# Attention over a dense adjacency mask: a fifth of the eight key groups is turned by DMA instead of TensorE, with SP's loads put ahead of its turns

## What is computed

```python
q = x @ Wq.T + bq;  k = x @ Wk.T + bk;  v = x @ Wv.T + bv
scores = jnp.where(adj > 0, q @ k.T / sqrt(128), -9e15)
att = softmax(scores, axis=-1) @ v
return layernorm(x + elu(att))          # no scale or shift, eps 1e-5
```

## Time and profile before

| | |
|---|---|
| median of 3 runs | 428.43 us |
| the profiled execution, its own time | 429.13 us |
| its span, first to last instruction | 427.3 us |
| TensorE busy | 416.2 us (97% of the span) |
| VectorE, ScalarE, GpSimd busy | 360.8, 353.8, 354.0 us |
| granted TensorE clock, mean | 0.998 |
| bytes moved by DMA | 104.77 MB, mean 245 GB/s |
| first and last turn issued by SP | 36.3 and 413.0 us |
| last load of adj issued | 386.4 us |

### The profile page before, as it was taken

How to read it: one execution, slowest core, us unless ns; L and a number is a source line. 1 busy time by engine, 2 the same in 40 slices (tenths; PEclk the granted TensorE clock), 3 DMA queues, 4 the chain that set the end, 5 groups by cost and what they waited for, 6 DMA issues and landing times.

```text
span 427.3 us, 11462 instructions
## 1 busy us (share of the span) xinstructions
PE 416.2 (97%) x3470; PEld 311.3 (73%) x3470; DVE 360.8 (84%) x677; ACT 353.8 (83%) x742; POOL 354.0 (83%) x644
## 2 busy tenths in 40 slices
PE   7997999999999999999999999999999999999994
PEld 6764777767777777777777777777777777777784
DVE  3889988888888898888888988888889888888784
ACT  4987788888888889888888898888888988888892
POOL 0596578988898889888988898889888988898875
PEclk9999999999999999999999999999999999999999
DMA  8944999899999999999999999999999999998550
GB/s 253 399 161 111 266 275 251 208 294 263 286 268 254 275 264 267 238 280 266 259 251 280 268 265 244 272 271 263 245 277 271 256 250 271 263 267 225 104 103 21
DMA packets 149794, 104.77 MB, mean 245 GB/s; under 512 B 132755, under 2 KB 141461, under 8 KB 141717
## 3 DMA queue, kind: packets, MB, share of 16 engines
q1 hardware_dynamic: 149344, 104.41, 92.0%
q10 hardware_dynamic: 436, 0.20, 0.2%
HBM read 69.47 MB, written 2.10 MB: 167 GB/s over the span
## 4 chain that ended last, share of the span: by engine, by line
POOL 58%; issue 18%; PE 10%; DMA 4%; ACT 3%; DVE 2%; POOLq 2%; SPq 2%; ACTq 0%; DVEq 0%
POOL p_rows L409 26%; POOL res L423 5%; POOL var_eps L445 4%; POOL rstd L447 4%; POOL att_sum L416 3%; POOL y L428 3%; POOL neg_mean L434 3%; POOL att L418 3%; POOL centred L436 2%; POOL expm L425 2%; DMA p_turned<-p_rows 2%; PE ps_out L967 2%; POOL y_out L451 2%; DMA x_rows<-in_x_dram 2%; POOL var L443 1%
## 5 line engine op out<-in xcount | busy, mean ns | idle before, releaser
L409 POOL TENSOR_TENSOR p_rows<-scores,p_rows 128x256 f16<-128x256 f32 x252 | 177.0, 733 | 7.3 <-ACT p_rows L566 7.1
L696 DVE CUSTOM_DVE_ANT_0 scores<-ps_scores,adj 128x1024 f32<-128x1024 f32 x128 | 155.9, 1218 | 13.0 <-issue 9.3
L549 ACT ACTIVATE scores<-scores,neg_max 128x1024 f32<-128x1024 f32 x128 | 145.8, 1139 | 3.5 <-DVE neg_max L706 3.5
L712 DVE TENSOR_TENSOR p_lo<-ps_t,p_hi 128x512 f16<-128x512 f32 x124 | 82.6, 686 | 28.4 <-ACT p_hi L558 28.3
L682 DVE TENSOR_SCALAR adj<-adj 128x1024 f32<-128x1024 int32 x128 | 103.5, 810 | 0.2
L928 PE MATMUL ps_scores<-k_hi,q_hi 128*128 128x512 f16 x256 | 97.0, 379 | 0.5 <-DVE max_parts L696 0.5
L929 PE MATMUL ps_scores<-k_lo,q_hi 128*128 128x512 f16 x256 | 97.0, 379 | 0.0
L930 PE MATMUL ps_scores<-k_hi,q_lo 128*128 128x512 f16 x256 | 97.0, 379 | 0.0
L967 PE MATMUL ps_out<-v_parts,p_turned 128*128 128x256 f16 x496 | 95.0, 273 | 0.4 <-DMA p_turned<-p_rows 0.3
L967 PE MATMUL ps_out<-v_parts,p_hi 128*128 128x256 f16 x496 | 95.1, 273 | 0.0
L969 PE MATMUL ps_out<-v_parts,p_lo 128*128 128x128 f16 x496 | 88.5, 219 | 0.0
(11 more groups left out here) (121 smaller groups left out, 479.8 us busy)
## 6 DMA issues: line engine op xcount, KB each, us to landing
adj<-in_adj_dram SPq DMA_DIRECT2D x63, 1024.0 KB, 5.3
out_dram<-y_out SPq DMA_DIRECT2D x32, 64.0 KB, 4.9
x_rows<-in_x_dram SPq DMA_DIRECT2D x4, 256.0 KB, 4.4
x_rows<-in_x_dram SPq DMA_DIRECT2D x2, 512.0 KB, 7.6
adj<-in_adj_dram SPq DMA_DIRECT2D x2, 512.0 KB, 7.4
p_turned<-p_rows SPq DMA_TRANSPOSE x63, 4.5
w_rows<-in_L_gnn_Wq_dram ACTq DMA_DIRECT2D x1, 64.0 KB, 2.7
w_rows<-in_L_gnn_Wk_dram ACTq DMA_DIRECT2D x1, 64.0 KB, 3.3
```

What stands on the lines that cost most here:

```text
L409: last = nc.gpsimd.tensor_tensor(p_rows[c][:, w:][:, cols], s_sb[s][:, c * PIECE:c * PIECE + w][:, cols], p_rows[c][:, 0:w][:, cols], ALU. ...
L549: nc.scalar.activation(s_sb[s][:, cols], s_sb[s][:, cols], ACT.Exp, bias=neg_max[:, s:s + 1], accum_out=p_sums[:, s, c:c + 1]).then_inc(ex ...
L696: nc.vector.tensor_tensor_reduce(out=s_sb[s][:, cols], in0=ps_scores[c % 2][:, :], in1=mask_sb[s][:, cols], scale=SCALE, scalar=-3.0e38, o ...
L712: nc.vector.tensor_tensor(p_lo[:, k, :], ps_t[bank_of(s, g)][:, :], p_hi[:, k, :], ALU.subtract).then_inc(plo_ready, 1)
```

## The change

Key group 4 (512 columns) moves from the TensorE way to the DMA way. `DMA_COLS` becomes (1024, 1536), so `p_rows[1]` holds 1536 high and 1536 low columns, and the turn of c = 1 moves 0.79 MB. TensorE's four transposes for group 4, ScalarE's `high_part(4)` and VectorE's `low_part(4)` go. In their place ScalarE makes the high part of the odd 512 columns from SBUF (`high_rows_odd`, step 6), and VectorE their low part from SBUF (`low_rows_odd`, step 7 after `row_max`). The turn of c = 1 waits for GpSimd's `rows_lo` and for VectorE's `rows_lo_odd`. GpSimd's own `low_rows` keep their size. `high_rows` of piece 1 moves from ScalarE's step 6 to step 4. SP's order in a period becomes: load of the second half for tile p+1, turn of c = 1, store, load of the first half for tile p+2, turn of c = 0. VectorE's four mask pieces of a period become pieces 2 and 3 of tile p and 0 and 1 of tile p+1. `PV_ORDER` and `T_AT` are fitted, the last tile keeps group 4 on TensorE.

```diff
-DMA_COLS = (PIECE, PIECE)
+DMA_COLS = (PIECE, PIECE + BANK)
-T_AT = {4: 6, 5: 7, 6: 8, 7: 10}
-PV_ORDER = (4, 0, 5, 6, 1, 7, 2, 3)
+T_AT = {5: 6, 6: 8, 7: 10}
+PV_ORDER = (5, 0, 1, 6, 7, 2, 3, 4)
...
             def turn(i, s, c):
                 sp.wait_ge(rows_lo, BY_DMA * i + c + 1)
                 sp.sem_inc(turn_begun, 1)
+                if c == 1:
+                    sp.wait_ge(rows_lo_odd, i + 1)
+                    sp.sem_inc(turn_begun, 1)
                 sp.dma_start_transpose(p_turned[c][s][:, :, :], p_rows[c][:, :]).then_inc(turned[c], 16)

             def period(p, n, head=True, turns_0=True, turns_1=True, stores=True, loads=True):
+                if head:
+                    load_half(p + 1, 1 - n, 1, False)
                 if turns_1:
                     turn(p - 2, n, 1)
-                if head:
-                    load_half(p + 1, 1 - n, 1, False)
                 if stores:
                     store(p - 4, n)
+                if loads:
+                    load_half(p + 2, n, 0, False)
                 if turns_0:
                     turn(p - 1, 1 - n, 0)
-                if loads:
-                    load_half(p + 2, n, 0, False)
...
+            def high_rows_odd(i, s, first):
+                act.wait_ge(exp_done, exp_count(i, 2))
+                if not first:
+                    act.wait_ge(turned[1], 16 * i)
+                nc.scalar.activation(p_rows[1][:, PIECE:PIECE + BANK], s_sb[s][:, 2 * PIECE:2 * PIECE + BANK],
+                                     ACT.Copy).then_inc(rows_hi_odd, 1)
...
-                    if j == (3 if not warm and p == 1 else 6) and has_1:
+                    if j == (3 if not warm and p == 1 else 4) and has_1:
                         high_rows(p - 1, 1 - n, 1, not warm and p == 1)
+                    if j == (5 if not warm and p == 1 else 6) and has_1:
+                        high_rows_odd(p - 1, 1 - n, not warm and p == 1)
...
+            def low_rows_odd(i, s):
+                w = DMA_COLS[1]
+                dve.wait_ge(rows_hi_odd, i + 1)
+                nc.vector.tensor_tensor(p_rows[1][:, w + PIECE:2 * w], s_sb[s][:, 2 * PIECE:2 * PIECE + BANK],
+                                        p_rows[1][:, PIECE:w], ALU.subtract).then_inc(rows_lo_odd, 1)
...
                     if j == 7 and has_scores:
                         row_max(p, n)
+                    if j == 7 and has_1:
+                        low_rows_odd(p - 1, 1 - n)
...
-                        if j == 1:
-                            mask_piece(p, n, 3)
-                        if j in (3, 5, 7) and makes_mask:
-                            mask_piece(p + 1, 1 - n, j // 2 - 1)
+                        if j in (1, 3):
+                            mask_piece(p, n, 2 + j // 2)
+                        if j in (5, 7) and makes_mask:
+                            mask_piece(p + 1, 1 - n, j // 2 - 2)
```

More of the change, by code:

```diff
@@ L173, in attention_kernel @@
         rows_lo = sem("rows_lo")
+        rows_hi_odd = sem("rows_hi_odd")
+        rows_lo_odd = sem("rows_lo_odd")
         turned = [sem(f"turned{c}") for c in range(BY_DMA)]
@@ L275, in attention_kernel, with turned_parts @@
         last_ps = dict(zip(range(LAST_PE, STEPS), last_ps + [ps_t[0][:, :], ps_t[1][:, :]]))
+        LAST_ACT = 4
+        def turned_parts(g, s):
+            c = 0 if g < 2 else 1
+            first = (g - 2 * c) * BLOCKS
+            half = DMA_COLS[c] // P
+            return (p_turned[c][s][:, first:first + BLOCKS, :], p_turned[c][s][:, half + first:half + first + BLOCKS, :])
         def last_high(g):
@@ L280, in last_high @@
                 return p_hi[:, g - FIRST_PE, :]
-            return p_turned[g // 2][1][:, g % 2 * BLOCKS:(g % 2 + 1) * BLOCKS, :].rearrange("p b r -> p (b r)")
+            return turned_parts(g, 1)[0].rearrange("p b r -> p (b r)")
         def last_low(g):
@@ L286, in last_low @@
                 return p_lo[:, g - FIRST_PE, :]
-            half = DMA_COLS[g // 2] // P + g % 2 * BLOCKS
-            return p_turned[g // 2][1][:, half:half + BLOCKS, :].rearrange("p b r -> p (b r)")
+            return turned_parts(g, 1)[1].rearrange("p b r -> p (b r)")
         block = ctx.enter_context(nc.Block())
@@ L407, in low_rows @@
                 for b in range(LOW_PARTS):
-                    cols = slice(b * w // LOW_PARTS, (b + 1) * w // LOW_PARTS)
+                    cols = slice(b * PIECE // LOW_PARTS, (b + 1) * PIECE // LOW_PARTS)
                     last = nc.gpsimd.tensor_tensor(p_rows[c][:, w:][:, cols], s_sb[s][:, c * PIECE:c * PIECE + w][:, cols],
@@ L560, in high_rows @@
             def high_rows(i, s, c, first):
-                w = DMA_COLS[c]
                 act.wait_ge(exp_done, exp_count(i, c))
@@ L565, in high_rows @@
                     act.wait_ge(turned[c], 16 * i)
-                nc.scalar.activation(p_rows[c][:, 0:w], s_sb[s][:, c * PIECE:c * PIECE + w], ACT.Copy).then_inc(rows_hi, 1)
+                nc.scalar.activation(p_rows[c][:, 0:PIECE], s_sb[s][:, c * PIECE:(c + 1) * PIECE], ACT.Copy).then_inc(rows_hi, 1)
+            def high_rows_odd(i, s, first):
[4 more added lines that the diff above has]
+                                     ACT.Copy).then_inc(rows_hi_odd, 1)
             def attention(i, s):
@@ L633, in _ @@
                     period(2 * pair + n, n)
-            high_part(LAST - 1, 0, 5, False)
             exp_piece(LAST, 1, 0, False)
@@ L734, in last_low_part @@
             def last_low_part(g):
-                if g < FIRST_PE:
+                if g < LAST_ACT:
                     dve.wait_ge(last_hi_dve, g - LAST_PE + 1)
                 else:
-                    dve.wait_ge(last_hi_act, g + 1 - FIRST_PE)
+                    dve.wait_ge(last_hi_act, g + 1 - LAST_ACT)
                 nc.vector.tensor_tensor(last_low(g), last_ps[g], last_high(g), ALU.subtract).then_inc(last_plo, 1)
@@ L789, in period @@
                             mask_piece(0, 0, c)
-                        for c in ((), (), (0,), (1, 2))[j // 2] if j % 2 == 1 else ():
+                        for c in ((), (), (0,), (1,))[j // 2] if j % 2 == 1 else ():
                             mask_piece(1, 1, c)
                     elif has_scores:
-                        if j == 1:
-                            mask_piece(p, n, 3)
-                        if j in (3, 5, 7) and makes_mask:
-                            mask_piece(p + 1, 1 - n, j // 2 - 1)
+                        if j in (1, 3):
+                            mask_piece(p, n, 2 + j // 2)
+                        if j in (5, 7) and makes_mask:
+                            mask_piece(p + 1, 1 - n, j // 2 - 2)
                     if j in rows_at:
@@ L832, in _ @@
             period(TILES - 1, 1, makes_mask=False)
-            low_part(LAST - 1, 0, 5)
             reciprocal(LAST - 1, 0)
@@ L837, in _ @@
                 low_part(LAST - 1, 0, g)
-            for g in range(LAST_PE, FIRST_PE):
+            for g in range(LAST_PE, LAST_ACT):
                 last_high_part(g)
@@ L841, in _ @@
             reciprocal(LAST, 1)
-            for g in range(FIRST_PE, STEPS):
+            for g in range(LAST_ACT, STEPS):
                 last_low_part(g)
@@ L950, in values @@
                     pe.wait_ge(plo_ready, PE_GROUPS * i + g - FIRST_PE + 1)
-                elif g % 2 == 0 or pv_count(0, g - 1) > pv_count(0, g):
+                elif g in (0, 2):
                     pe.wait_ge(turned[g // 2], 16 * i + 16)
@@ L964, in values @@
                     else:
-                        high = p_turned[g // 2][s][:, g % 2 * BLOCKS + b, :]
-                        low = p_turned[g // 2][s][:, DMA_COLS[g // 2] // P + g % 2 * BLOCKS + b, :]
+                        high, low = (part[:, b, :] for part in turned_parts(g, s))
                     nc.tensor.matmul(ps_out[s][:, 0:2 * D], high, v_parts[:, k, :],
@@ L975, in last_transposes @@
                 if g > 5:
-                    pe.wait_ge(plo_ready, PE_GROUPS * (LAST - 1) + g - FIRST_PE + 1)
+                    pe.wait_ge(plo_ready, PE_GROUPS * LAST)
                 for b in range(BLOCKS):
@@ L1031, in _ @@
             transposes(LAST - 1, 0, 6, False)
-            values(LAST - 1, 0, 4, False)
+            values(LAST - 1, 0, 5, False)
             values(LAST - 1, 0, 0, False)
@@ L1035, in _ @@
             transposes(LAST - 1, 0, 7, False)
-            values(LAST - 1, 0, 5, False)
             values(LAST - 1, 0, 6, False)
@@ L1039, in _ @@
             last_transposes(3)
-            for g in (7, 2, 3):
+            for g in (7, 2, 3, 4):
                 values(LAST - 1, 0, g, False)
-            for g in range(FIRST_PE, STEPS):
+            for g in range(LAST_ACT, STEPS):
                 last_transposes(g)
```

## The result

The changed kernel takes 496.15 us (median of 4 runs, 495.97 to 498.68) against 428.54 us beside it: a ratio of 1.159, 95% interval 1.157 to 1.161. The forecast was 451 us, 433 to 460. The direction was right, the size was not: the loss is three times what I forecast. The profiled execution has a span of 494.4 us.

What follows compares the result with a forecast made beforehand. TensorE bounds the loop at 12.19 us a period. The DMA ring becomes 11.81 + 0.91 + 0.30 = 13.02 us, +0.83 over 28 periods; less 0.9 on TensorE, 428.4 + 22.3 = 451 us, range 433 to 460.

Steps and rivals of the forecast that it cites:

- TensorE's 0.43 us a period: On TensorE, four transposes removed: 0.43 us less a period, 11.76 us if TensorE still sets it.
- The move itself gives the DMA engines nothing: SP's queue: load, turn, load, turn before and after, so reordering loads and turns changes nothing for the DMA engines.
- the store's place: SP's queue: the store now delays a load behind a turn; 0 to 0.62 us a period, taken as 0.30.
- The chain through the moved load: Rival: turn lands, TensorE, masked piece 3, load, next turn behind it; 12.3 us a period, 431 us; chance 0.07.
- The turn's extra 0.26 MB: DMA: the turn of c = 1 grows from 0.52 to 0.79 MB, adding 0.91 us a period, 1.22 at most.
- The low rows' place behind the row maximum: VectorE: odd low rows come about 0.7 us later than GpSimd's part, SP's turn waiting for them; nothing in the sum.
- my count of 28 periods: Whole kernel: 350/12.19 = 28.7 periods between first turns and last load, 28 counted, each 0.83 us longer.
- The masks at zero: VectorE's mask pieces: each needs its half of adj later than before, none becomes late; zero cost.
- GpSimd as the bound: Rival: VectorE's new subtraction holds GpSimd for 0.6 us; period 12.46 us, 435 us; chance 0.12.
- What I named as signs: If right: TensorE 90% busy, waits for `p_turned` or at `high_rows`, c = 1 turns over 4 us, SP's period 13.0 us.
- the ring: DMA queue: two turns and two loads a period, 11.81 us, becoming the bound at 13.02 us; chance 0.62, 442 to 460.

Runs made afterwards that it cites:

- run 3: The changed kernel with SP's order of before and the high rows of piece 1 back at ScalarE's step 6: 455.79 us, ratio 1.064.
- run 8: The kernel of run 3 with each load of the loop bringing only 256 of its 2048 columns: 432.86 us, ratio 1.010.
- run 7: The changed kernel with each load of the loop bringing only 256 of its 2048 columns: 440.48 us, ratio 1.028.
- run 4: The kernel before with SP's new order alone, each load ahead of its turn: 447.19 us, ratio 1.045.
- run 9: The kernel of run 4 with the store moved to between the second load and the turn of c = 0: 441.76 us, ratio 1.031.
- run 2: The changed kernel with the high rows of piece 1 back at ScalarE's step 6, SP's new order kept: 477.12 us, ratio 1.118.
- run 1: The changed kernel with SP's order of before, the high rows of piece 1 still at step 4: 456.63 us, ratio 1.065.
- run 5: The kernel of run 3 with VectorE's odd low rows at the head of step 7, ahead of masked piece and row maximum: 452.38 us, ratio 1.056.
- run 11: The kernel before with the changed order of the mask pieces alone: 428.61 us, ratio 1.001.

## Why the prediction was wrong

**TensorE's 0.43 us a period** was right as an amount of work (four transposes take 0.44 us in run 3's chain) and never arrived: something else set the pace in every version, run 8 included.

**"The move itself gives the DMA engines nothing"** is the step that failed first. I compared the cyclic order of the queue, load, turn, load, turn, which is the same before and after, and concluded that only the store's place mattered. But a queue's order also says who waits for whom. Before, a load was issued right behind a turn and had a start of 3 us on the next one while SP waited for low rows: behind the load at 203.62 comes

```profile
206.73 3.01 SPq L314 DMA_TRANSPOSE p_turned<-p_rows  x1
```

After, the load goes out 0.5 to 1.1 us in front of the turn, on a masked piece that is itself at the end of TensorE's period, and the turn lands after 7.4 us instead of the 5.5 it takes with small loads (run 7). With short turns the order alone is 19 us (run 4), of which the store's place is about 5 (run 9; I had 0.3 us a period, 8 us).

**The chain through the moved load** was a rival, at 431 us and a chance of 0.07. It is what happened, at 14.4 us instead of 12.3. The load's issue to the turn's landing was 8.0 us in my sum and is 8.4 (217.14 to 225.55). The way back from the landing to the end of the masked piece was 4.3 us and is 5.8 (225.55 to 231.34): I followed TensorE from the values of step 5, and did not follow ScalarE, where the moved high rows (1.0 us) and the exponential of piece 2 (1.2 us) stand in front of TensorE's transposes. I had not costed the move from step 6 to step 4 at all. Run 2 puts it at 19 us with the new order, runs 1 and 3 at 1 us with the old one. I also closed the rival with a price worked out to a tenth from parts that the trace of before could not show together, and gave it no upper end.

**The turn's extra 0.26 MB** was near: 0.91 us forecast on a ring of 11.81 us, 12.72; where the chains are short and the order is old, the period is 12.87 us (run 5). At the backlog's 272 GB/s instead of 289 the estimate would have been 0.96 us, 12.77. No run changes the size of the turn alone, and SP waited 1.9 us for low rows in the stretch from which I had the 11.81, so part of the agreement may be luck. Had the change kept SP's order and ScalarE's step, my sum without the store's term would have given 442 us; the runs gave 452 with the odd low rows early and 456 with them late. The low rows' place behind the row maximum, at nothing in my sum, is the 3 us between the two. By my count of 28 periods 12.87 us a period would make 446.5 us; run 5 has 6 us more, so the count or something outside it was off too, which was not traced.

**The masks at zero** were right (run 11).

**GpSimd as the bound** did not come in the changed kernel, where GpSimd is busy for 182.7 of 248 us. That VectorE's subtraction with two SBUF inputs holds GpSimd is borne out in run 5, at 0.46 us where the rival had 0.6. The Trainium skill ("SBUF — State Buffer", Who interferes with whom) says that a VectorE instruction with two SBUF inputs contends with a GpSimd instruction that reads SBUF. The trace agrees: 3.02 us instead of 2.56 for four of them.

**What I named as signs**: turns over 4 us (5.60 and 5.73 for c = 1 in SP's timeline), waits for `p_turned` and for ScalarE at `high_rows` came; TensorE at 90% (it is 85%) and SP's period of 13.0 us did not. The signs that came fit the ring and the chain alike and could not tell them apart. The DMA share does not either: 1.00, 1.03 and 0.96 stand beside 12.8, 13.6 and 14.3 us (runs 4 and 2, and the changed kernel). It says little of the bytes, as two half-microseconds of the changed kernel show, 0.91 at 131 GB/s and 1.14 at 442:

```profile
226.00:226.50 0.50, 0.50 (x8) 0.36 (x6) 0.26 (x1) 0.50 (x1) 0.00 (x0) 1.00 0.91 131
...
228.00:228.50 0.50, 0.50 (x5) 0.49 (x6) 0.00 (x0) 0.50 (x3) 0.23 (x2) 1.00 1.14 442
```

The cause of the 68 us, then: with the old order and step the longer turn, its odd low rows and its earlier reader cost 27 us (run 3), of which 23 go when the loads are small (run 8); the new order adds 21 on top (run 2 against run 3); the earlier step adds 19 more, only because the turn now lands after ScalarE wants it. Open stays how the 27 us divide, why the new order moves fewer bytes in the same time even with SP always busy (run 4), and what run 8's schedule lacks.

## What to carry to other kernels

A transfer queue has two prices: how full it is, and what the transfer that someone waits for is queued behind. Put a bulk load behind the transfer that is on the path, not in front of it, even if it could be issued earlier: in each of the three pairs of runs that differ in SP's order alone, the loads in front lost time, 19, 21 and 40 us. And when an instruction that waits for a transfer moves up in an engine's order, follow everything it steps in front of: the price is zero while the transfer lands early and the whole wait as soon as it doesn't, so such a move and one that delays the transfer must be costed together, round the loop until the chain meets itself.

## What the hardware showed that I had not expected

The instruction of a turn on SP lasts longer the more is queued in front of it. For 0.52 MB it took 2.0 us with an empty queue, 2.8 to 3.3 us in the steady state of the kernel before and 4.9 to 5.3 us right behind a load (run 4). Its own size counts too: the 0.79 MB turn took about 3.6 us behind a small load (run 7) and 5.2 to 6.2 us behind a full one (run 5). For turns of one size it is thus a reading of the queue's depth, and a better one here than the DMA share. And a small transfer in a queue can cost more than its bytes: the half of run 4's ring with the 64 KB store took 6.75 us against 6.06. Moving that store elsewhere won 5 us in the whole kernel (run 9), less than a third of these 0.69 us a period.
